# Block scales with an accumulator, and new orders of the five queues in a fused attention and FP4 MLP kernel

## The reference

```python
Q, K, V = xpos(X @ W_Q), xpos(X @ W_K, downscale=True), X @ W_V    # 256 x 256 weights
p = softmax(Q @ K.T, axis=-1) * 0.9 ** abs(n - m)                  # 1024 x 1024 a batch
x = layernorm(X + p @ V)
q = lambda t: blocks of 16: scale = max(max|t| / 6, 1e-12), t / scale rounded to the FP4 grid, * scale
h = silu(q(x) @ q(w_gate).T) * (q(x) @ q(w_up).T)                  # 704 columns
out = layernorm(x + q(h) @ q(w_down).T)
```

## Time and profile before

| what | value |
| --- | --- |
| median of 3 runs (lowest, highest) | 1103.22 us (1102.05, 1105.62) |
| the profiled execution | 1102.92 us, span 1101.0 us |
| mean granted TensorE clock | 0.977 of full speed |
| DMA | 111.26 MB, mean 101 GB/s |
| steps 56 to 63 and the drain begin | 885.31 us, 1025.45 us |
| the chain of waits, shares by engine | POOL 29%, DVE 29%, issue 26%, PE 8%, ACT 4% |

### The profile page before, as it was taken

The page is one execution under the profiler, slowest core; times in us unless marked ns, Lnnn a source line. Parts: engine busy times, 40 slices in busy tenths (PEclk is TensorE's granted clock), DMA queues, the critical chain, the costliest instruction groups (busy, mean ns, idle before and its releaser), DMA issues.

```text
span 1101.0 us, 20402 instructions
## 1 busy us (share of the span) xinstructions
PE 996.8 (91%) x6002; PEld 879.3 (80%) x6002; DVE 901.7 (82%) x1874; ACT 636.2 (58%) x1575; POOL 829.0 (75%) x1034
## 2 busy tenths in 40 slices
PE   8989999999999999999999999999999997778755
PEld 7778888888788888888788888788888886667655
DVE  7878889888888898888888898888888886676554
ACT  3636666566566665665666665665666555453422
POOL 6968787887888788787888788787978785564423
PEclk9999999999999999999999999999999998898988
DMA  7123243233423234243423234243433222221100
GB/s 284 44 88 117 80 139 115 78 120 114 141 85 122 88 112 139 67 135 101 140 92 120 89 103 143 80 132 95 131 94 127 90 77 82 72 73 63 44 10 15
DMA packets 116111, 111.26 MB, mean 101 GB/s; under 512 B 12576, under 2 KB 93728, under 8 KB 114080
## 3 DMA queue, kind: packets, MB, share of 16 engines
q1 hardware_dynamic: 115312, 108.91, 30.9%
q10 hardware_dynamic: 688, 1.05, 0.3%
HBM read 69.53 MB, written 40.37 MB: 100 GB/s over the span
## 4 chain that ended last, share of the span: by engine, by line
POOL 29%; DVE 29%; issue 26%; PE 8%; ACT 4%; DMA 2%; SPq 1%; POOLq 0%; DVEq 0%; ACTq 0%
POOL prob L2314 5%; POOL rot_a L2212 5%; POOL h L2199 4%; DVE rot_b L1606 3%; DVE rot_a L1606 3%; POOL xv L2199 3%; DVE turned L1701 2%; DVE hsc L1623 2%; DVE hsc L1618 2%; POOL xt_l L2228 2%; POOL rs L2273 2%; DVE h L1669 2%; POOL h_last L2205 2%; DVE xv L1717 2%; DVE xv L1724 2%
## 5 line engine op out<-in xcount | busy, mean ns | idle before, releaser
L2199 POOL TENSOR_TENSOR h<-h,hsc 128x704 f32<-128x704 f32 x126 | 168.5, 1337 | 57.8 <-DVE h L1675 34.5
L607 PE MATMUL ps_oy<-v_h,pt_h 128*128 128x256 f32 x512 | 152.9, 299 | 38.0 <-POOL pt_l L2286 37.5
L2314 POOL TENSOR_TENSOR prob<-prob,decay_t 128x512 f32<-128x512 f32 x128 | 164.7, 1294 | 0.0
L607 PE MATMUL ps_g<-wgu_h,xqt_h 128*128 128x480 f32 (+1 forms) x380 | 150.6, 396 | 8.9 <-DVE h L1643 5.3
L609 PE MATMUL ps_oy<-v_h,pt_l 128*128 128x256 f32 x512 | 147.5, 288 | 0.0
L608 PE MATMUL ps_oy<-v_l,pt_h 128*128 128x256 f32 x512 | 147.3, 288 | 0.0
L609 PE MATMUL ps_g<-wgu_h,xqt_l 128*128 128x480 f32 (+1 forms) x380 | 142.8, 376 | 0.0
L608 PE MATMUL ps_g<-wgu_l,xqt_h 128*128 128x480 f32 (+1 forms) x380 | 142.7, 376 | 0.0
L607 PEld LDWEIGHTS ps_oy<-v_h,pt_h 128*128 128x128 f32 x512 | 99.7, 195 | 50.0 <-POOL pt_l L2286 45.0
L1168 ACT ACTIVATE ps_oy<-xv 128x256 f32<-128x256 f32 x63 | 24.5, 389 | 166.7 <-DVE r L1762 149.9
L1682 DVE TENSOR_TENSOR ht_l<-ps_t,ht_h 128x512 fp32r<-128x512 f32 x126 | 56.4, 485 | 62.3 <-ACT ht_h L1257 62.3
(11 more groups left out here) (274 smaller groups left out, 3237.7 us busy)
## 6 DMA issues: line engine op xcount, KB each, us to landing
parking<-turned SPq DMA_DIRECT2D x122, 256.0 KB, 2.0
landing<-parking SPq DMA_DIRECT2D x488, 64.0 KB, 2.0
rope_t<-rope SPq DMA_DIRECT2D x15, 1024.0 KB, 5.6
xres<-x SPq DMA_DIRECT2D x64, 128.0 KB, 2.1
out<-yout SPq DMA_DIRECT2D x63, 128.0 KB, 2.0
xin<-x_t SPq DMA_DIRECT2D x14, 512.0 KB, 4.2
first_rope<-rope SPq DMA_DIRECT2D x2, 512.0 KB, 8.1
decay_t<-decay SPq DMA_DIRECT2D x1, 960.0 KB, 12.0
```

What stands on the lines that cost most here:

```text
L607: pe.matmul(dst, a_h, b_h, start=(start and i == 0), stop=False)
L2199: return tt(blocks(dst), blocks(src), sc[:, which, at:at + n].unsqueeze(2).to_broadcast([P, n, QB]), ALU.mult)
L2314: tt(prob[:, keys], prob[:, keys], decay_t[:, lo:lo + CW], ALU.mult).then_inc(decayed, 1)
```

## The change

`block_scales` gets `accum_out`: the operation also writes out an accumulator, to a buffer `unread` of two columns that nothing reads. All other edits move calls in the written lists; no call is added or taken away. In `step(s)`: on PE, steps of the last batch and of kind j = 1, 5 begin with `scores(now, 0)` and `down(five)`, then `values_product_first(two)`; rotation steps have `scores(now, 1)` ahead of it; j = 7 has both halves of the scores ahead of `down`; j = 3 has both halves of the values product ahead of `x1_transposes`, and both have `h_transposes` behind the second `gate_up`. SP's kinds change as the diff shows. ACT, DVE and POOL have new lists for each kind: rotation steps and j = 7 put `turn(one, 0)` first on DVE, and the former put `second_residual` ahead of `landed_low`, and `landed_low(one)` ahead of `r1_inverse` on POOL; j = 7 puts `row_max(now)` ahead of `second_residual`; j = 1, 5 put both turns behind `x_grid`; the last batch has `turn(one, 0)` behind the scales and `first_residual` ahead of `xqt_low`. In the drain `probs_high(last)` goes ahead of `r1_mean(last - 1)` and `r2_mean(last - 4)` (ACT), `gated` and `silu` of the first part ahead of `probs_low` (DVE), `down(last - 3)` ahead of `x1_transposes(last - 1)` (PE), and `x_quantised(last - 1)` ahead of `h_units(last - 2)` (POOL). The core of the diff (SP; PE for j = 0, 7, 3, the last batch and the drain; ACT's drain; block scales; DVE's last batch and drain; POOL's drain):

```diff
         hsc = sb("hsc", [P, 3, F // QB])
+        unread = sb("unread", [P, 2])
         mhalf = sb("mhalf", [P, 1])
...
                 now, one, two, three, four, five, six = (s - lag for lag in range(7))
                 if s % NT in (0, 2, 4, 6):
                     park(one, 0)
+                    load_x(s)
                     store(six)
                     land(one, 0)
                     park(one, 1)
-                    load_x(s)
+                    land(one, 1)
                     load_residual(one)
+                elif s % NT == NT - 1:
+                    store(six)
+                    park(one, 0)
+                    park(one, 1)
+                    load_residual(one)
+                    land(one, 0)
                     land(one, 1)
-                elif s % NT == NT - 1:
+                elif s % NT == 3:
+                    store(six)
                     park(one, 0)
-                    store(six)
                     park(one, 1)
                     land(one, 0)
+                    land(one, 1)
                     load_residual(one)
-                    land(one, 1)
-                elif s % NT == 3:
+                else:
+                    store(six)
+                    load_rope(s)
                     park(one, 0)
-                    store(six)
-                    land(one, 0)
                     park(one, 1)
                     load_residual(one)
+                    land(one, 0)
                     land(one, 1)
-                else:
-                    park(one, 0)
-                    store(six)
-                    park(one, 1)
-                    land(one, 0)
-                    load_rope(s)
-                    land(one, 1)
-                    load_residual(one)
...
                     scores(now, 0)
                     down(five)
                     projection()
+                    scores(now, 1)
                     values_product_first(two)
-                    scores(now, 1)
...
                     gate_up(three, 2)
                 elif c_v is not None and rotation_is_urgent(s):
                     scores(now, 0)
+                    scores(now, 1)
                     down(five)
-                    scores(now, 1)
                     projection()
                     values_product_first(two)
                     x1_transposes(three)
                     values_product_second(two)
-                    h_transposes(four, 0)
                     projected()
                     gate_up(three, 0)
                     gate_up(three, 1)
+                    h_transposes(four, 0)
                     h_transposes(four, 1)
                     gate_up(three, 2)
                 elif c_v is not None:
...
                     down(five)
                     values_product_first(two)
                     projection()
+                    values_product_second(two)
                     x1_transposes(three)
-                    values_product_second(two)
                     scores(now, 1)
-                    h_transposes(four, 0)
                     projected()
                     gate_up(three, 0)
+                    gate_up(three, 1)
+                    h_transposes(four, 0)
                     h_transposes(four, 1)
-                    gate_up(three, 1)
                     gate_up(three, 2)
                 elif s // NT == NB - 1:
+                    scores(now, 0)
+                    down(five)
                     values_product_first(two)
-                    down(five)
-                    scores(now, 0)
                     values_product_second(two)
                     x1_transposes(three)
                     scores(now, 1)
...
             h_transposes(last - 4, 1)
             gate_up(last - 3, 2)
             down(last - 4)
-            prob_transposes(last, 0)
-            prob_transposes(last, 1)
             values_product_first(last - 1)
             values_product_second(last - 1)
             x1_transposes(last - 2)
+            prob_transposes(last, 0)
+            prob_transposes(last, 1)
             gate_up(last - 2, 0)
             gate_up(last - 2, 1)
-            gate_up(last - 2, 2)
             h_transposes(last - 3, 0)
             h_transposes(last - 3, 1)
+            gate_up(last - 2, 2)
             values_product_first(last)
             values_product_second(last)
+            down(last - 3)
             x1_transposes(last - 1)
-            down(last - 3)
             gate_up(last - 1, 0)
             gate_up(last - 1, 1)
             gate_up(last - 1, 2)
+            x1_transposes(last)
             h_transposes(last - 2, 0)
             h_transposes(last - 2, 1)
-            x1_transposes(last)
             last_gate_up(0)
             last_gate_up(1)
...
             tanh(last - 3, 2)
-            landed_high(last - 1, 0)
+            output(last - 5)
+            landed_copied(last - 1)
             first_norm(last - 2)
             landed_high(last - 1, 1)
-            landed_copied(last - 1)
-            output(last - 5)
             x_magnitude(last - 2)
             h_magnitude(last - 3)
             x1_high(last - 2)
+            probs_high(last, 1)
+            probs_high(last, 0)
+            r1_mean(last - 1)
+            tanh(last - 2, 0)
+            r1_squares(last - 1)
+            tanh(last - 2, 1)
+            h_high(last - 3, 0)
+            first_norm(last - 1)
             r2_mean(last - 4)
-            r1_mean(last - 1)
+            tanh(last - 2, 2)
             r2_squares(last - 4)
-            r1_squares(last - 1)
-            probs_high(last, 0)
-            probs_high(last, 1)
-            tanh(last - 2, 0)
-            first_norm(last - 1)
-            h_high(last - 3, 0)
             h_high(last - 3, 1)
-            tanh(last - 2, 1)
-            tanh(last - 2, 2)
             output(last - 4)
             x_magnitude(last - 1)
             x1_high(last - 1)
             h_magnitude(last - 2)
...
 
-            def block_scales(sc, done):
+            def block_scales(sc, done, which=0):
 
                 nc.vector.tensor_scalar(sc[:, 0, :], sc[:, 2, :], TIES_DOWN / 6.0, MIN_SCALE * TIES_DOWN, ALU.mult,
-                                        ALU.max).then_inc(done, 1)
+                                        ALU.max, accum_out=unread[:, which:which + 1]).then_inc(done, 1)
...
             def x_scales(i):
                 if live(i):
                     wait(dve, xmax_done, i + 1)
-                    block_scales(xsc, xscale_done)
+                    block_scales(xsc, xscale_done, 1)
 
...
+                elif s // NT == NB - 1:
                     x_scales(three)
-                    turn(one, 0)
                     h_max(four)
                     x_reciprocals(three)
                     h_scales(four)
+                    turn(one, 0)
+                    h_reciprocals(four)
                     row_inverse(two)
-                    h_reciprocals(four)
                     second_residual(five)
                     landed_low(two)
                     x_shift(three)
                     x_grid(three)
                     turn(one, 1)
                     h_shift(four)
+                    first_residual(two)
+                    xqt_low(three)
                     h_grid(four)
-                    xqt_low(three)
-                    first_residual(two)
-                    v_low(c_v, 0)
-                    v_low(c_v, 1)
                     row_max(now)
-                    h_low(four, 0)
                     gated(three, 0)
                     silu(three, 0)
                     gated(three, 1)
+                    silu(three, 1)
+                    h_low(four, 0)
                     h_low(four, 1)
-                    silu(three, 1)
                     gated(three, 2)
                     x_max(two)
                     silu(three, 2)
...
             h_max(last - 3)
+            x_max(last - 2)
             h_scales(last - 3)
             x_scales(last - 2)
             x_reciprocals(last - 2)
             h_reciprocals(last - 3)
-            row_inverse(last - 1)
+            second_residual(last - 4)
             landed_low(last - 1)
-            second_residual(last - 4)
             x_shift(last - 2)
             x_grid(last - 2)
             h_shift(last - 3)
             xqt_low(last - 2)
             h_grid(last - 3)
             first_residual(last - 1)
+            gated(last - 2, 0)
             row_inverse(last)
+            silu(last - 2, 0)
             probs_low(last, 0)
             probs_low(last, 1)
-            gated(last - 2, 0)
-            silu(last - 2, 0)
             h_low(last - 3, 0)
+            gated(last - 2, 1)
+            x_max(last - 1)
+            silu(last - 2, 1)
+            gated(last - 2, 2)
             h_low(last - 3, 1)
-            gated(last - 2, 1)
-            silu(last - 2, 1)
-            x_max(last - 1)
+            silu(last - 2, 2)
             x_scales(last - 1)
             x_reciprocals(last - 1)
```

(30 more changed lines are left out.)

318 lines of the change are left out of this document (159 added, 159 removed).

## The result

| | before | changed |
| --- | --- | --- |
| median us of four runs each (lowest, highest) | 1103.22 (1102.05, 1105.62) | 996.58 (994.89, 998.63) |
| span of the profiled execution, mean granted clock | 1101.0, 0.977 | 995.0, 0.998 |

The change makes the kernel faster: ratio 0.9032 [0.9009, 0.9055], 106.6 us. Forecast were 59 us, with a range that ended at 1024 us. The sign and the places were right; the size was not.

A forecast was written before the change was run, and what follows sets the result against it. TensorE, with matmuls in flight for 91% of the span, was taken as the bound, with only its gaps removable. Last batch -28, steady steps -24, drain -7 and start 0 sum to -59: 1102.9 to 1044 us, range 1024 to 1074.

The forecast's parts named there:

- Last batch: Steps 57 to 62: scores and down ahead of the first values product shorten steps from 17.63 to 13.5 us, -28 us.
- the guess that DVE would share the bound: Last batch: DVE and TensorE both nearly full, so the step settles between 12.5 and about 14.5 us, taken as 13.5.
- Slower: SP: Rival, kinds j = 1, 5, 7: landings queued behind load_residual stall ACT, 60 us over 20 steps, 1104 to 1110 us; chance 0.06.
- Steady steps: Steps before the last batch: pt_l and xv waits shrink, DVE gains from the scales; -24 us, bounds -46 and some +5.
- the discount: Steady steps: of 28.4 us of xv waits only 13 taken as gained, and 6 of the total given back.
- The walk: Steady steps: following the new orders through a step of each kind, which says all of TensorE's waits go.
- all waits go: Rival, whole kernel: every wait goes, -34 - 45 - 12 gives 1012 us; chance 0.07.
- the head of kinds j = 1, 5: Steady steps: the pt_l wait at the head of 14 steps, 1.16 us each and 0.16 with it, all goes: -17.5 us.
- The form of the scales: Block scales: with the accumulator output they no longer wait for GpSimd, at a price of 0.1 us each, 13 us.
- Drain: From 1025 to 1101 us: moved items remove waits of ACT, DVE and TensorE; -7 us, bounds -14 and +3.
- the halving: Drain: at most 4 + 10 us go, but half is taken since much work only moves earlier: -7 us.
- The three waits named: Drain: ACT's r2_mean 4.18 us, DVE's second_residual(last - 3) 9.00, TensorE's x1_transposes(last - 1) 8.70; at most 4 + 10 go.

The follow-up runs named there:

- undo_head: Changed kernel with values_product_first(two), down(five), scores(now, 0) in the old order at TensorE's step heads (j = 1, 5, last batch): 1032.47 us, ratio 0.9351.
- orders_only: Changed kernel without the accumulator output in the block scales, all new lists kept: 1036.75 us, ratio 0.9398 to the kernel before.
- accum_only: Kernel before with the accumulator output in the block scales and nothing else: 1085.35 us, ratio 0.9845.
- pe_lists: Kernel before with TensorE's new lists alone in steps 3 to 55, plain scales: 1120.22 us, ratio 1.0157.
- drain_five: Kernel before with five drain edits: down, x_quantised, probs_high moves, plus scores and down before the first values product, and h_quantised earlier: 1086.14 us, ratio 0.9854.

## Why the prediction was wrong, step by step

**Last batch: right.** Forecast -28 (bounds -34 and -16), measured -31.3. The loop through `pt_l` was the limit, the head of the step broke it (`undo_head`: steps of 16.7 us), and the step fell to TensorE's own work, 12.53 us against the 12.5 worked out. Over the six steps it is 12.9 us, since steps 57 and 58 still take 13.1 and 14.1. Off by up to one was the guess that DVE would share the bound and make it 13.5: the gate chain at the end of DVE's step runs into the next one without holding TensorE, and DVE is busy for 11.68 of 12.60 us. The waits ahead of the steps were not all of 3.3 us: 1.16 stood ahead of step 57 and 5.53 ahead of step 58. SP's landings were hidden there, as said. ACT's waits for them ahead of `landed_high` in the whole kernel, of which it had none before:
```profile
ACT pt_h L1146 <- DMA landing<-parking: 7.6, 15, 1.2
```
All 15 lie in steps 6 to 54, most of them right behind a step j = 1 or 5, where the rival "Slower: SP" put them: 7.6 us against its 60.

**Steady steps: the failed step is the discount.** The walk said that all waits go; I wrote that I didn't believe it in full, took 13 of 28.4 us for `xv` and gave 6 back, and came to -24 (the terms give -24.5). Measured are -44.5, next to the -46 of the bound, and -3.7 in the start, for which 0 was forecast: it comes with the new lists of the first steps (70.0 us to step 4 in `orders_only`, 73.6 in `accum_only`). DVE's 108.4 of 124.9 us was read as a reason for a wait to come back; but with the scales free that load is 104.54 us, and in a batch of 118.26 it holds TensorE for no longer than the 0.4 us of the `xv` waits. The rival "all waits go", 1012 us with a chance of 0.07, was the nearest.

Two terms of the sum rest on a reason that did not hold. The -17.5 us for the head of kinds j = 1, 5 was priced from TensorE's order alone. Within the full change its size is right (16, `undo_head`), but with TensorE's lists alone the wait only moves to the second half of the values product and the pair of steps gains 0.27 us (`pe_lists`, in all 18 us slower). It gains only with the lists of DVE, ACT and POOL that come with it. And the scales were said to lie off TensorE's path but for `xv`, 13 us or less: alone they are worth 18, and on top of the new lists 1036.75 - 996.58 = 40, since the new lists put them beside POOL's work (764 ns for a median one). The 40 us of hold-up were read from the order of before; in `orders_only` the scales take 46.2 + 34.2 = 80.4 us, 61 more than at their best times (64 x 0.161 + 63 x 0.136 = 18.9).

**The form of the scales: right.** No hold-up in 127, and 0.08 us for the second instruction. The Trainium skill, page "SBUF — State Buffer", section "Who interferes with whom", has the form with the accumulator outside the rule that excludes GpSimd, which no row of before showed. The trace agrees: at most 202 ns now, though 100 of the 127 begin inside a long instruction of POOL.

**Drain: the failed steps are the halving, and that the sum has only these waits.** Forecast -7, bound -14, measured -26.5. The three waits named were right and are worth 12.4 us together, near the bound (4 + 10), not half of it. Two more were in the trace and not named for the drain: the 3.33 us wait at the head of step 63, which the forecast had in its last batch, and the 6.49 us wait for `h`, both for POOL; they give 3.4 (`drain_five`), 1.3 of it behind the start of step 63. And the sum had no term for the clock, which it did count in the last batch. The granted clock of this stretch rose from 0.86 to 0.97, and TensorE's busy time for the same products fell from 58.70 to 52.59 us, 6 of the 26.5. In the changed kernel nothing longer than 2.0 us is left on TensorE there. Timeline of PE, ahead of the `gate_up` of tile 62, against 1.62 us there before, and 8.70 ahead of that tile's `x1_transposes`:
```profile
964.55 0.49 PE L608 MATMUL ps_g<-wgu_h,xqt_h 128*128 128x480 f32 x1 [0.92 <-DVE xqt_l L1731]
```
and of DVE, `second_residual(last - 3)`, which waited 9.00 us:
```profile
963.45 0.42 DVE L1763 TENSOR_TENSOR r<-ps_oy,x 128x256 f32<-128x256 f32 x1 [0.77 <-PE ps_oy L804]
```
The remaining 12.9 us (28.7 - 15.8) come from the other moves of the drain's lists. The time from the first values product of tile 63 to the end is 55.0 us before, 47.4 with the five edits and 38.9 changed, so most of what is open lies behind that product; `drain_five` still has its waits of 3.09 and 4.29 us there, and a granted clock of 0.87 against 0.95. Which moves do it was not tried one by one and stays open.

**The sum.** -31.3 - 48.2 - 26.5 = -106.0, against -59: 3 us of the 47 missing are the last batch's, 24 the steady part's and the start's, 20 the drain's.

## What to carry to other kernels

Price an order of one queue together with those of the queues it meets: TensorE's new lists cost 18 us alone, and in company their head alone carries 16 of the steady steps' gain. The sign of it in a trace is an engine idle for an item while ready ones stand behind it. Where a walk says that all waits go and the engine that should bring them back still has over 10% of room (108.4 of 124.9 us), take the walk seriously: here it was the better forecast, and the doubt belonged in the range. And look for small operations that two engines serialise (0.14 us of work, up to 1.27 us long): their cost depends on the order, so it must be priced anew for the order that follows.
